# Two-block vision kernel: fc2 of the first block in two halves, with the turns of the last pair between and behind them

## The reference

```python
q, k, v = qkv[0], qkv[1], qkv[2]                      # 7x7 windows, 12 heads of 8
attn = einsum('whqd,whkd->whqk', q, k) / clip(|q| |k|, 1e-06) / clip(tau, 0.01)
attn = softmax(attn + bias + mask)
out = (attn @ v) @ proj_w + proj_b
x = shortcut + ln(out)
h = gelu(x @ fc1_w + fc1_b) @ fc2_w + fc2_b           # hidden width 384
x = x + ln(h)
```

## Time and profile before

| | us |
|---|---|
| median of 3 runs | 7351.25 |
| lowest and highest of them | 7350.71 and 7351.86 |
| the profiled execution | 7357.88 |
| span of its trace | 7355.7 |
| granted TensorE clock over it | 0.99 |

### The profile page before, as it was taken

How to read it: one execution, slowest core, us unless ns; L and a number is a source line. 1 busy time by engine, 2 the same in 40 slices (tenths; PEclk the granted TensorE clock), 3 DMA queues, 4 the chain that set the end, 5 groups by cost and what they waited for, 6 DMA issues and landing times. The chain is left out here.

```text
span 7355.7 us, 316783 instructions
## 1 busy us (share of the span) xinstructions
PE 7116.4 (97%) x113246; PEld 5479.5 (74%) x113246; DVE 5960.6 (81%) x12718; ACT 6066.2 (82%) x11264; POOL 5785.7 (79%) x6469
## 2 busy tenths in 40 slices
PE   6999999999999999999999997999999999999999
PEld 4777777777777777777777775777777777777777
DVE  4898888888888888888888875777777777777776
ACT  4888888888888888888888876887887887887888
POOL 3899999899998999989999885666666666666665
PEclk9999999999999999999999998999999999999999
DMA  0111111111111111111111101111111111111111
GB/s 19 30 30 30 30 30 30 30 29 31 30 30 29 30 30 30 30 30 30 30 30 30 29 24 25 30 30 29 29 30 29 30 30 29 30 30 29 30 29 27
DMA packets 342621, 214.37 MB, mean 29 GB/s; under 512 B 265624, under 2 KB 341144, under 8 KB 341144
## 3 DMA queue, kind: packets, MB, share of 16 engines
q1 hardware_dynamic: 341146, 194.49, 10.9%
HBM read 78.66 MB, written 77.07 MB: 21 GB/s over the span
## 5 line engine op out<-in xcount | busy, mean ns | idle before, releaser
L873 POOL TENSOR_TENSOR swin_score<-swin_score,swin_top 113x588 f32<-113x588 f32 x1024 | 1178.8, 1171 | 72.2 <-DVE swin_top L738 68.8
L1561 POOL TENSOR_TENSOR plain_k_heads<-plain_k_hat,plain_head_mask 96x512 f32<-96x512 f32 x392 | 398.9, 1037 | 914.5 <-DVE plain_k_hat L1452 914.5
L484 PE MATMUL swin_ps_probs<-swin_ident,swin_prob 113*128 113x113 f32 x6144 | 1014.5, 274 | 62.1 <-ACT swin_probT L622 9.8
L622 ACT ACTIVATE swin_probT<-swin_ps_probs 128x339 f32<-128x339 f32 x1792 | 805.2, 449 | 303.2 <-PE swin_ps_probs L484 250.8
L484 PEld LDWEIGHTS swin_ps_probs<-swin_ident,swin_prob 113*128 113x128 f32 x6144 | 627.2, 141 | 496.9 <-ACT swin_probT L622 239.0
L733 DVE TENSOR_TENSOR swin_score<-swin_ps_scores,swin_bias_tab 113x588 f32<-113x588 f32 x1024 | 740.5, 765 | 71.6 <-PE swin_ps_scores L474 38.6
L738 DVE TENSOR_REDUCE swin_top<-swin_score 113x12 f32<-113x588 f32 x1024 | 730.3, 754 | 0.0
L628 ACT ACTIVATE swin_prob<-swin_score 113x588 f32<-113x588 f32 x1024 | 713.8, 697 | 0.1
L1439 DVE TENSOR_REDUCE plain_top<-plain_ps_scores 128x6 f32<-128x384 f32 x784 | 432.6, 552 | 277.2 <-PE plain_ps_scores L1214 277.2
L566 PE MATMUL swin_ps_dense<-swin_w_fc,swin_hid 128*98 128x96 f32 x6144 | 584.5, 252 | 1.4 <-ACT swin_hid L689 1.4
L1340 ACT ACTIVATE plain_probT<-plain_ps_probs 128x384 f32<-128x384 f32 x784 | 382.2, 488 | 225.6 <-PE plain_ps_probs L1238 225.4
(11 more groups left out here) (189 smaller groups left out, 21291.4 us busy)
## 6 DMA issues: line engine op xcount, KB each, us to landing
swin_k_heads<-swin_k_hat SPq DMA_DIRECT2D x1024, 36.8 KB
plain_x_in<-between_blocks SPq DMA_DIRECT2D x784, 48.0 KB, 2.2
out_dram<-plain_x SPq DMA_DIRECT2D x784, 48.0 KB, 2.0
swin_x_in<-in_x SPq DMA_DIRECT2D x224, 136.5 KB
between_blocks<-swin_x SPq DMA_DIRECT2D x224, 136.5 KB
swin_x_in<-in_x SPq DMA_DIRECT2D x224, 19.5 KB
between_blocks<-swin_x SPq DMA_DIRECT2D x224, 19.5 KB
swin_x_in<-in_x SPq DMA_DIRECT2D x224, 2.6 KB
```

Source lines behind the costliest of these rows:

```text
L484: last = nc.tensor.transpose(psP[:, n * QT:(n + 1) * QT], prob[0:QT, p, 2 * hp:2 * hp + 2, :].rearrange('p h k -> p (h k)'), ident[0:QT, 0 ...
L622: nc.scalar.activation(to, psP[:, 0:3 * QT], ACT.Copy).then_inc(did['probT'], 1)
L873: nc.gpsimd.tensor_tensor(view, view, bcast(top[0:QT, p, :], 2, WIN), ALU.subtract).then_inc(did['shifted'], 1)
```

## The change

PE: `output` is split by pairs. The first half makes pairs 0 and 1 of fc2 and raises no semaphore, the second makes pairs 2 and 3 and raises `fc2_made`. `turn_probs(-1, 3, 0)` stands between the halves, and `turn_probs(-1, 3, 1)`, which stood between `hidden(-3, 0)` and `hidden(-3, 1)`, stands behind the second half, ahead of all of `hidden`. ACT: `copy_turned(-1, 3, 0)` goes ahead of `log_norms(1)`, and `copy_turned(-1, 3, 1)` goes between `log_norms(1)` and `invert_norms(1)`; before, it stood behind `exponentials(0, 1)`. No instruction is added or taken away. The second block is as it was.

```diff
-                    def output(d, bank):
+                    def output(d, h, bank):
                         if exists(g + d, groups):
                             pe.wait_ge(did['hid'], upto(g + d, CHUNKS - 1, CHUNKS))
-                            for p in range(PAIRS):
+                            for p in (2 * h, 2 * h + 1):
                                 for c in range(CHUNKS):
                                     last = nc.tensor.matmul(...)
-                            last.then_inc(did['fc2_made'], 1)
+                            if h == 1:
+                                last.then_inc(did['fc2_made'], 1)
...
-                    output(-4, C)
+                    output(-4, 0, C)
                     turn_probs(-1, 3, 0)
+                    output(-4, 1, C)
+                    turn_probs(-1, 3, 1)
                     free(('proj_read', -2), ('sq_norm', 1, 1, 2), ('v_heads', 1), ('hid', -4, 0, CHUNKS))
                     hidden(-3, 0, A)
-                    turn_probs(-1, 3, 1)
...
                     square_y(-2, A)
+                    copy_turned(-1, 3, 0)
                     log_norms(1)
-                    copy_turned(-1, 3, 0)
+                    copy_turned(-1, 3, 1)
                     invert_norms(1)
                     exponentials(0, 1)
-                    copy_turned(-1, 3, 1)
                     act.preload_act_table_set(GELU_SET)
```

## The result

| | before | after |
|---|---|---|
| median, us | 7351.56 (4 runs) | 7499.85 (4 runs) |
| lowest and highest | 7350.71 and 7355.69 | 7492.56 and 7512.97 |
| the profiled execution | 7357.88 | 7492.56 |
| span of its trace | 7355.7 | 7490.4 |
| ratio after / before | | 1.0203, 95% interval 1.0185 to 1.022 |

The kernel became slower by 2.0%, some 148 us. The forecast was slower by 23 us: the sign is right, the size is a sixth of what came, and the time lies far outside the range of 7348 to 7397.

The account below looks back on a forecast made before the run. No engine is dense; a ring of hand-overs with two tied branches bounds the body. Loop 224 x (0.28 - 0.16) = +26.9, outside 32 x -0.11 = -3.5, together +23.4 on 7351.25: 7375 us, range 7348 to 7397.

Parts of the forecast that it names:

- The two branches: From fc2 through ACT's copies and PE's turns; from ACT's invert_norms through scale_k and DVE. They meet at DVE's copy, tied.
- the slack of 0.16: On DVE ahead of the bias addition, which waits for PE's scores in the loop: 0.16 us to spare, none behind it.
- The price of a set of turns in fc2: PE time of a set of turns between fc2's halves: 0.28 us, bounds 0.23 and 0.44.
- invert_norms 0.29 later: On ACT, invert_norms behind the second copy starts at 10.46 instead of 10.18: forecast 0.28 us later.
- Both removed waits: PE's waits of 0.31 ahead of turn (3, 1) and 0.39 ahead of turn (0, 0) go, giving about 0.4 us slack.
- the bodies outside the loop: DVE's slack there is 0.39, more than the delay of 0.28: 32 bodies 0.11 us shorter each, -3.5 us.
- scale_k starts 0.28 later, and so q_hat and z_var: On DVE, the delay of invert_norms passes on to these: 0.28 us later, scale_k's idle growing from 0.73 to 1.0.
- POOL then goes on as before: POOL's shift moves by 0.12 us with DVE's first reduction, the rest of POOL unchanged; costed at nothing.
- Expected delay of the bias addition in the loop: On DVE, 0.28 less slack of 0.16: 0.12 us later, making each of 224 loop bodies 0.12 longer, +26.9 us.
- The rivals: All of 0.28 passed on, 7423 (with the price's far end 0.09); faster, to 7303 (0.11); cancelled, within 0.2% (0.12).

Follow-up runs that it names:

- e12_before_swapped: The kernel before the change, with square_z put ahead of rstd_y on POOL; 7354.5 us, ratio 1.0003 to before.
- e10_square_first: The changed kernel with square_z put ahead of rstd_y on POOL; 7276.01 us, ratio 0.9896 to before.
- e3_invert_first: The changed kernel with invert_norms put ahead of the second copy (copy_turned(-1, 3, 1)) on ACT; 7254.82 us, ratio 0.9871 to before.
- e6_one_pad: The changed kernel with one small addition (98x4) put on POOL between rstd_y and square_z; 7540.11 us, ratio 1.0251 to before.
- e4_pe_only: PE's part of the change alone, with ACT in the order of the kernel before; 7316.63 us, ratio 0.9953 to before.
- e2: The kernel before the change, without POOL's addition of epsilon to the variance, so z_sq starts earlier; 7416.98 us, ratio 1.009 to before.
- e9: The changed kernel without POOL's addition of epsilon to the variance, so z_sq starts 0.28 us earlier; 7410.52 us, ratio 1.0078 to before.
- e5: The changed kernel with POOL's z_sq made for one pair of four and DVE's sum reading it four times; 7359.62 us, ratio 1.0007 to before.
- e1: The changed kernel with two small additions (98x4) put on POOL between rstd_y and square_z; 7399.29 us, ratio 1.0064 to before.

## Why the prediction was right and wrong

**Right.** The two branches, their tie and the slack of 0.16: e12_before_swapped (branch two alone shortened: nothing), e10_square_first and e3_invert_first (with branch one shortened too: gains). The price of a set of turns in fc2: the two turns start 1.33 apart, and with the first half's 1.07 from fc2's start they give 2.40 for the forecast's 2.39, so a set costs 2.40 - 2.11 = 0.29. I took 0.28; the estimated 0.32 by the weight-load rule of the Trainium skill would have been 0.03 too much. invert_norms 0.29 later, and why. Both removed waits are gone, as no idle stands ahead of the turns at 2012.38 and 2014.30. The bias addition no longer waits for the scores, so the slack was taken. And the bodies outside the loop: where k_hat keeps its 0.62, in e6_one_pad, they take 277.15 - 260.40 = 16.75 for before's 16.87. That is 0.12 less, and 0.11 less was the forecast.

**Wrong.** The step that failed is "scale_k starts 0.28 later, and so q_hat and z_var". It carried k_hat's 0.62 along as if it were fixed, where 1.11 was measured, and the cover "POOL then goes on as before" looked at POOL as a queue and not as a neighbour of DVE. With the measured length the sum closes. Expected delay of the bias addition in the loop: 0.12 + 0.49 = 0.61, and 14.05 - 13.44 = 0.61 was measured. The additions and reductions behind it then took 19.49 - 16.80 = 2.69 for 16.18 - 13.44 = 2.74, so 0.55 to 0.56 arrives at the copy, and the body grows by 17.20 - 16.65 = 0.55.

Over the loop, 224 x 0.55 = 123.2. From the loop's first k_hat to the one behind its last (371.99 to 4120.85 before, 372.83 to 4247.81 after) the time grew by 126.1; two of the six bodies at a granted clock of 0.91 lie there, and at 1.5 us each they are the other 3. Outside the loop the spans grew by 7.5 where 3.5 less was forecast. In an ordinary body there k_hat takes 1.20:

```profile
267.13 1.20 DVE L819 SCALAR_TENSOR_TENSOR swin_k_hat<-swin_qk,swin_inv_tau,swin_sq_norm 96x392 f32<-96x392 f32 x1 [0.93 <-ACT swin_sq_norm L673]
```

That is 0.58 over its 0.62, and the forecast's -0.11 becomes -0.11 + 0.58 = 0.47. From this k_hat to the next it is 284.46 - 267.13 = 17.33, and before has 303.89 - 287.02 = 16.87 in this stretch: 0.46 was measured. So the sign of the forecast was turned by the same instruction. The sum of 7.5 is smaller than 26 such bodies would make: four bodies at the lower clock add 6, while the first five are 7.4 us shorter together than before's and before has a few single longer ones; why is not shown.

**The rivals** all erred with the forecast: each of them was about how much of 0.28 is passed on. None had a longer instruction in it, so the range, built from them, could not reach 7500. The delay was 0.28 to 0.29, and what decided was that k_hat stood only 0.15 ahead of z_sq.

**What rows of before would have told.** k_hat's most of 1008 ns beside a median of 623; q_hat at twice its least; POOL's z_sq with a start 0.15 behind a start that was to move by 0.28. How long it would get was in the rows as well: q_hat, second to z_sq, ended 0.43 behind it. By the 0.41 of the runs (last section) z_sq ends 11.30 + 0.83 = 12.13, so k_hat ends near 12.54 and lasts 1.10; 1.11 was measured.

**Left open.** Who is first when two starts are 0.01 or 0.02 apart (e4_pe_only and e6_one_pad below). Why the three executions of after without a trace are longer than the fourth. And whether ACT's list is all that sets the 16.30 of e3_invert_first.

## What to carry to other kernels

Before moving an instruction by tenths of a microsecond, look at what runs at its new place on an engine that it has been seen to wait for (here POOL, for DVE), and take a duration from the row only together with its least and most over the run: half of it can be a wait that no idle shows. In a ring with two tied branches, shortening one shows nothing until the other is shortened too, so try the parts in pairs. When removing work makes a kernel slower, compare the order of starts across engines first. And before a difference is put down to a wait alone, look at the granted clock of single bodies: more idle on PE went with more bodies at the lower clock here.

## What was not expected of the hardware

- **When the second one ends.** For k_hat and q_hat (DVE, 96x392, two SBUF inputs; 0.62 and 0.56 alone) against z_sq and y (POOL, 98x384; 0.83 alone), the DVE instruction that comes second ends 0.41 to 0.43 behind POOL's end: after 14.89 and 15.30, e2 2.07 and 2.49, e9 16.33 and 16.74, e6 16.75 and 17.17, q_hat of before 12.46 and 12.89. In e5 (12.27 and 12.70) it ends where its own 0.63 takes it. POOL's, coming second, ends 0.69 behind DVE's end: before 11.77 and 12.46, e1 13.55 and 14.24, e5 12.70 and 13.39. So of k_hat 0.62 - 0.41 = 0.21, of q_hat 0.56 - 0.43 = 0.13 and of POOL's 0.83 - 0.69 = 0.14 do not show up behind the other's end; only the rest does. The Trainium skill ("SBUF — State Buffer", Who interferes with whom) has the second blocked until the first is done, and the measured ends come earlier than that by these amounts.
- **It chains.** In after, z_sq delays k_hat, k_hat delays y (1.15), y delays q_hat (1.18).
- **One small POOL instruction was no obstacle.** Beside y_rstd (98x4, 1.02 us) k_hat and q_hat keep their lengths in e10_square_first; the other way, y_rstd grew to 1.37 in e12_before_swapped beside two DVE instructions.
- **Starts 0.01 or 0.02 apart don't tell the order.** At 0.10 and more the earlier one was first (z_sq 13.09 behind q_hat 12.99 in e1_pad). In e6_one_pad k_hat's start is 0.02 ahead of z_sq's and it is second; in e4_pe_only q_hat's is 0.01 behind z_sq's and it is first:

```profile
2011.94 0.56 DVE L825 TENSOR_TENSOR swin_q_hat<-swin_qk,swin_sq_norm 96x392 f32<-96x392 f32 x1
...
2011.93 1.25 POOL L919 TENSOR_TENSOR swin_z_sq<-swin_z 98x384 f32<-98x384 f32 x1
```
